# The router's logits as four fp32 products of rows copied as they are, in place of twelve products of fp16 halves

## The chip, the cores and the metric

The kernel runs on one core of one Trainium2 chip. The metric is the device time of one execution in microseconds. Engines are named as the profile names them: PE (TensorE), PEld (its weight loads), DVE (VectorE), ACT (ScalarE), POOL (GpSimd), SP (SyncE); ACTq, POOLq and the like are the instruction queues of these engines.

## The reference, cut to what matters

Two blocks of a transformer on x of 4 x 512 rows of 512 numbers (a sequence mixer, a Hadamard feed-forward, cross-attention over 4 x 1024 context rows, and a mixture of 32 experts of which each row takes 8). The change touches the router of the last part:

```python
x = x + _L1_xattn_ref(_layernorm(x, axis=-1), ctx_2048, mask_BxS2_bk0)
x = x + _L1_ffn_ref(_layernorm(x, axis=-1), L1_ffn_gate_kernel, ...)
...
    x2d = hidden_states.reshape(T, D)                 # T = 2048 rows of D = 512
    router_logits = x2d @ gate_kernel                 # gate_kernel: 512 x 32, fp32
    routing_weights = jax.nn.softmax(router_logits, axis=-1)
    routing_weights, selected_experts = jax.lax.top_k(routing_weights, TOP_K)
    ...
    # rows sorted by expert, gate, up and down products of each expert's rows, weighted sum back
```

## The kernel before, in words

The work is written out by hand, engine by engine, as one program for each engine; only semaphores order one against another. The 2048 rows are 16 tiles of 128 rows (`NT` = 16, `TT` = 4 to each of 4 batches).

From about 612 us on, the cross-attention and the router run in one loop over the tiles. In its turn t the program of PE does, in this order: `probs(t)` (eight transposes of the attention weights, L1848), `logits(t - 2)` (L1827), `scores(t + 1)` (24 products of 128x512), `rank(t - 2)` (three small products, L1839 to L1841), `readout(t)` (24 products of 128x512), with `query_tile` and `router_tile` (four transposes each, L1814) put between its pieces. `router_tile(t - 1)` transposes the normalised rows of tile t - 1 into PSUM. From there ACT writes them to SBUF as fp16 (`router_hi`, L776) and DVE writes what the rounding left, as fp16 too (`router_lo`, L1334). `logits` then is, for each of the four pieces of 128 of the 512 numbers, three products with the high and low halves of the gate matrix (`gkh`, `gkl`), which ACT and DVE make once before the loop (L783, L1395); PE waits for `gkl` before its first scores. A product here is a weight load of 128x128 and a matmul that streams 32 columns.

In the same turn DVE does `probs_lo` (L1306), the root of the layer norm interleaved with the choice of the 8 experts of tile t - 2 (`tile_root_and_choose`, L1012 to L1032 and L1339 to L1367), the normalised rows (L1065), `scores_max(t + 1)` (L1300), `place_first` and `place` (L1381 to L1391, which give the rows' places `POS`), then `query_lo`, `router_lo`, `readout_sum` (L1324). ACT does `probs_hi` (L761), `router_exp` (L780), `exp_tile` (L755), `query_hi`, `router_hi`. POOL waits for `POS` and issues eight scatters of the tile's rows into HBM (L560). The last two tiles (a = 14, b = 15) are written out behind the loop.

From about 872 us on, the experts' loop goes over 159 tiles of rows sorted by expert, 8 tiles to a turn. ACT begins each turn with two loads of a table into registers (`rows_at`, `experts_due`, L104): the places of 12 tiles, and for 16 tiles the count at which their expert has landed. SP writes rows of padding behind the last row of each expert (`pad_expert`, L494) and loads the weights of the experts, four of them at a time (L488).

Of the kernel before, what the change touches and what calls it, by code (L numbers as in the profile page):

```python
# [15 lines left out]
F16 = mybir.dt.float16  # L16
# [90 lines left out]

def wait_apart(eng, sem, value, passed):


    eng.wait_ge(sem, value)
    eng.sem_inc(passed, 1)


def build(nc, a_x, a_ctxT, a_ctxr, a_kv, a_mask, a_winT, a_woutT, a_cols, a_rows, a_wug, a_wdT,
          a_gk, a_exp, a_ident, a_had, a_hadf, a_tri, d_exp, d_kv, d_row, d_down, a_out):
    ctx = ExitStack()
    with ctx:
# [28 lines left out]
        gkh = sb("gkh", [P, KC, NE], F16)  # L147
        gkl = sb("gkl", [P, KC, NE], F16)
# [99 lines left out]
        rh = [f16(SUMX, 0, (KC, P)), f16(HT, 1024, (KC, P))]  # L248
        rl = [f16(SUMX, KC * P // 2, (KC, P)), f16(HT, 1280, (KC, P))]
# [80 lines left out]
        s_rt, s_rhi, s_rlo = sem("router_tile_transposed"), sem("router_tile_hi"), sem("router_tile_lo")  # L330
        s_gkh, s_gkl, s_rc0, s_rcz = sem("router_hi"), sem("router_lo"), sem("router_consts"), sem("row_pads_cleared")
# [20 lines left out]
        def _(sp):  # L352
# [152 lines left out]
            for e in range(WP):  # L505
                pad_expert(e, 16 * e)
            sp.wait_ge(s_tab, 1)
            with sp.Fori(1, NE // WP) as i:
                for h in range(WP):
                    pad_expert(i * WP + h, i * (16 * WP) + 16 * h)  # L510
                    wait_apart(sp, s_wl, i * (16 * WP) + 16 * h, s_spassed)

                    done = sp.value_load(TCUM[0:1, bass.ds(i * WP + (h - WP), 1)], min_val=1, max_val=NTILE + 1)
                    sp.wait_ge(s_ed, done)
                    load_expert(i * WP + h, h)
# [5 lines left out]
        def _(pool):  # L521
# [68 lines left out]
            with pool.Fori(0, LOOPS) as it:  # L590
                start = load_ints(pool, "expert_start", TAB[0:1, 4, bass.ds(it * U, U)], 0, NTILE)
                for u in range(U):
                    add(it * U + u, u, start[u])
            start = load_ints(pool, "last_start", TAB[0:1, 4, bass.ds(LOOPS * U, REST)], 0, NTILE)
# [5 lines left out]
        def _(act):  # L600
# [181 lines left out]
            act.wait_ge(s_gk, 16)  # L782
            act.activation(gkh[:, :, :], gk, ACT.Copy, scale=E_S).then_inc(s_gkh, 1)  # L783
# [9 lines left out]
            for t in range(NT - 1):  # L793
                probs_hi(t)
                if t == 0:
                    for b in range(3, B):
                        count_keys(b)
                if t > 1:
                    router_exp(t - 2)
                exp_tile(t + 1)  # L800
                if t + QA < NT:
                    query_hi(t + QA)
                if t:
                    router_hi(t - 1)
# [3 lines left out]
            for t in range(NT - 2, NT):  # L808
                router_hi(t)
                router_exp(t)  # L810
# [18 lines left out]
            def experts_due(name, t, count):  # L829
                return load_ints(act, name, TAB[0:1, 1, bass.ds(t, count)], 16, 16 * NE)  # L830
# [21 lines left out]
            with act.Fori(0, LOOPS) as it:  # L852
                rows, due = rows_at("tile_row", it * U + 4, U + 4), experts_due("tile_due", it * U, U + 8)
                for u in range(U):
                    t = it * U + u

                    hidden_hi(t, u % 2)
                    tile_hi(t + 2, u % 2, due[u + 2])
                    if u < TOPK - LEAD:
                        act.wait_ge(s_add[LEAD + u], LANDED)  # L860
                    load_tile((u + LEAD) % U, t + (V + LEAD - U + 1), rows[u + LEAD - 4], due[u + LEAD])
                    tile_silu(t + 1, (u + 1) % 2)
# [13 lines left out]
        def _(dve):  # L876
# [166 lines left out]
            def tile_root_and_choose(m, n, cols, t):  # L1043

                tile_root_start(m, n, cols)
                logits_scale(t)
# [322 lines left out]
            def choose(t):  # L1369

                logits_scale(t)
# [22 lines left out]
            dve.wait_ge(s_gkh, 1)  # L1394
            v.scalar_tensor_tensor(gkl[:, :, :], gk, E_S, gkh[:, :, :], ALU.mult, ALU.subtract).then_inc(s_gkl, 1)  # L1395
# [7 lines left out]
            for t in range(NT - 1):  # L1403
# [36 lines left out]
                if t:  # L1440
                    router_lo(t - 1)
# [57 lines left out]
            router_lo(a)  # L1499
            last_moments(1)  # L1500
            root_start(1)
            logits_scale(a)
# [15 lines left out]
            router_lo(b)  # L1518
# [93 lines left out]
        def _(pe):  # L1612
# [247 lines left out]
            pe.wait_ge(s_gkl, 1)  # L1860
# [198 lines left out]
```

## Time and profile before

| | |
|---|---|
| median of 3 runs | 1451.21 us (1450.37 to 1453.27) |
| span of the profiled execution | 1474.3 us |
| PE busy | 1382.7 us (94%) |
| DVE busy | 1022.1 us (69%) |
| ACT, POOL busy | 505.4 us, 383.7 us |
| matmuls, weight loads | 7525, 7526 |
| mean granted TensorE clock | 0.977 |

The profile gives one execution, and its span is the only time that it records for it; it is 23.1 us above the median of the runs that were timed without a profile. Nothing else is known of what lies around the span. A row of the timeline gives start and duration; a matmul's start is a measured time, its end is modelled, so the pace of products is read from start to start. The brackets at a row's end say how long the engine had been idle before it and what ended that.

### The profile page before, as it was taken

What the parts mean: (1) busy time and instruction counts of PE and PEld (TensorE: products, weight loads), DVE (VectorE), ACT (ScalarE), POOL (GpSimd) and SP (SyncE); (2) the same over time, 40 slices, a digit from 0 to 9 for tenths busy, and PEclk for the clock granted to TensorE, in tenths of its full rate; (3) what the DMA queues carried; (4) which work ended last, traced back from release to release, by engine and by line L of the source; (5) the groups of instructions that cost most, each with busy time, mean ns of one, the idle gap of its engine ahead of it and who ended that gap; (6) DMA issues with size and microseconds to landing.
All of it is one profiled execution on the core that took longest, in us unless ns stands there. A gap on an engine that the chain in (4) does not pass through costs nothing.

```text
span 1474.3 us, 26984 instructions
## 1 busy us (share of the span) xinstructions
PE 1382.7 (94%) x7525; PEld 753.2 (51%) x7526; DVE 1022.1 (69%) x2467; ACT 505.4 (34%) x916; POOL 383.7 (26%) x313
## 2 busy tenths in 40 slices
PE   4799999999999999999999559999999999999997
PEld 3344444444444444455444236666666666666664
DVE  7879857976895656688776536666666666666664
ACT  1454543444435343422222113333333333333332
POOL 1000000000000000025556543444344344344443
PEclk9899999999999999999999769999999999999999
DMA  9975776766767778836748668889999888989785
GB/s 370 396 262 193 263 256 213 247 197 205 241 209 237 235 254 286 280 119 251 284 195 294 242 227 216 223 218 260 246 246 234 221 229 228 247 223 222 148 162 84
DMA packets 132696, 345.04 MB, mean 234 GB/s; under 512 B 15008, under 2 KB 19616, under 8 KB 125728
## 3 DMA queue, kind: packets, MB, share of 16 engines
q1 hardware_dynamic: 73488, 206.72, 41.6%
q0 software_dynamic: 34640, 85.74, 25.2%
q10 hardware_dynamic: 24512, 51.89, 10.8%
q8 instruction: 27, 0.44, 0.1%
q14 instruction: 29, 0.24, 0.0%
HBM read 192.68 MB, written 151.62 MB: 234 GB/s over the span
## 4 chain that ended last, share of the span: by engine, by line
PE 68%; DVE 16%; DMA 4%; issue 4%; ACT 3%; another core or an unknown queue 2%; ACTq 1%; SPq 1%; DVEq 0%; POOLq 0%
PE PS L1671 17%; PE PS L1673 17%; PE PS L1672 17%; PE PS L1933 5%; PE PS L1961 2%; PE PS L1962 2%; DMA split_experts<-HT 2%; DMA CST<-in_kv 1%; PE PS L1950 1%; DVE EX L1300 1%; PE PS L1951 1%; DVE EX L1306 1%; DVE nw L1027 1%; DMA X<-in_x 1%
## 5 line engine op out<-in xcount | busy, mean ns | idle before, releaser
L587 POOL DMA_INDIRECT out<-BIG,EX x159 | 247.2, 1555 | 354.9 <-issue 153.4
L1671 PE MATMUL PS<-BIG 128*128 (+1 forms) x795 | 269.5, 339 | 5.0 <-DVE BIG L1572 3.3
L1672 PE MATMUL PS<-BIG 128*128 (+1 forms) x795 | 269.5, 339 | 0.0
L1673 PE MATMUL PS<-BIG 128*128 (+1 forms) x795 | 269.5, 339 | 0.0
L1671 PE MATMUL PS<-HT,BIG 128*128 128x512 f16 (+1 forms) x512 | 194.1, 379 | 3.0 <-DVE HT L1101 1.4
L1672 PE MATMUL PS<-HT,BIG 128*128 128x512 f16 (+1 forms) x512 | 194.0, 379 | 0.0
L1673 PE MATMUL PS<-HT,BIG 128*128 128x512 f16 (+1 forms) x512 | 194.0, 379 | 0.0
L560 POOL DMA_INDIRECT rows_by_expert<-HT,POS x128 | 124.9, 976 | 122.6 <-DVE POS L1391 88.1
L1672 PE MATMUL PS<-BIG,EX 128*128 128x512 f16 (+1 forms) x376 | 143.8, 382 | 1.1 <-issue 1.1
L824 ACT ACTIVATE BIG<-PS 128x256 f16<-128x256 f32 x159 | 61.1, 384 | 243.3 <-PE PS L1951 229.0
L1673 PE MATMUL PS<-BIG,EX 128*128 128x512 f16 (+1 forms) x376 | 143.6, 382 | 0.4 <-issue 0.4
L1671 PE MATMUL PS<-BIG,EX 128*128 128x512 f16 (+1 forms) x376 | 143.8, 382 | 0.0
L1576 DVE SCALAR_TENSOR_TENSOR BIG<-PS,BIG 128x192 f32<-128x192 f32 x159 | 56.8, 357 | 104.1 <-ACT BIG L820 95.1
L1567 DVE SCALAR_TENSOR_TENSOR BIG<-PS,BIG 128x512 f16<-128x512 f32 x159 | 109.9, 691 | 23.8 <-ACT BIG L816 14.0
L1585 DVE TENSOR_SCALAR BIG<-PS,BIG 128x512 f32<-128x512 f32 x159 | 119.4, 751 | 0.0
L650 ACT ACTIVATE HT<-HT 128x1280 f16<-128x1280 f32 x64 | 81.2, 1268 | 94.5 <-DMA split_experts<-HT 94.3
L552 POOL MEMSET HT<- 128x105 f32 x1 | 0.2, 186 | 422.7 <-DMA split_experts<-HT 422.7
L1673 PEld LDWEIGHTS PS<-BIG 128*128 128x128 f16 x795 | 78.3, 98 | 59.6 <-issue 1.6
L820 ACT ACTIVATE BIG<-PS 128x192 f32<-128x192 f32 x159 | 52.7, 331 | 158.4 <-PE PS L1673 133.0
L1933 PE MATMUL PS<-ident,BIG 128*128 128x128 f32 x636 | 96.8, 276 | 7.7 <-issue 7.7
L1671 PEld LDWEIGHTS PS<-BIG 128*128 128x128 f16 x795 | 78.2, 98 | 50.1 <-issue 9.9
L816 ACT ACTIVATE BIG<-PS 128x512 f16<-128x512 f32 x158 | 93.4, 591 | 25.3 <-remote 25.3
(264 smaller groups left out, 2218.0 us busy)
## 6 DMA issues: line engine op xcount, KB each, us to landing
BIG<-rows_by_expert ACTq DMA_DIRECT2D x159, 280.0 KB
HT<-in_experts SPq DMA_DIRECT2D x64, 640.0 KB, 4.6
BIG<-split_experts SPq DMA_DIRECT2D x32, 1152.0 KB
split_experts<-HT SPq DMA_DIRECT2D x96, 320.0 KB, 2.2
CST<-in_kv SPq DMA_DIRECT2D x64, 256.0 KB, 4.7
split_context<-RT SPq DMA_DIRECT2D x64, 256.0 KB, 4.5
BIG<-split_context SPq DMA_DIRECT2D x7, 2048.0 KB
rows_by_expert<-X SPq DMA_DIRECT2D x32, 280.0 KB
```

Source lines behind the costliest of these rows:

```text
L560: pool.indirect_dma_start(d_row, bass.IndirectOffsetOnAxis(ap=POS[:, t % ZN, c:c + 1], axis=0), ZR[:, t % ZN, :], None).then_inc(s_ids[t % ...
L587: pool.indirect_dma_start(a_out, bass.IndirectOffsetOnAxis(ap=IDY[:, u % V:u % V + 1], axis=0), yt[u % V], None, compute_op=ALU.add).then_ ...
L650: act.activation(eoh, est[h], ACT.Copy, scale=E_S).then_inc(s_eh, 1)
L816: act.activation(xh[p], PS[:, p, :].rearrange("p (k n) -> p k n", n=P), ACT.Copy, scale=H_S).then_inc(s_xh, 1)
L824: act.activation(eah[p], PS[:, 4, 0:2 * P], ACT.Copy).then_inc(s_ah2, 1)
L1567: v.scalar_tensor_tensor(xl[p], PS[:, p, :].rearrange("p (k n) -> p k n", n=P), H_S, xh[p], ALU.mult, ALU.subtract).then_inc(s_xl, 1)
L1576: v.scalar_tensor_tensor(ea[p][:, 0:M], PS[:, 2 + p, M:2 * M], 1.0 / (H_S * E_S), eg[p], ALU.mult, ALU.mult)
L1585: v.tensor_scalar(yt[u % V], PS[:, 5 + u % 2, :], xg[u][:, bass.ds(e + D, 1)], None, ALU.mult).then_inc(s_y, 1)
L1671: mm(out, lh, rh, start=first, stop=False)
L1672: mm(out, lh, rl, start=False, stop=False)
L1673: return mm(out, ll, rh, start=False, stop=last_group)
L1933: last = nc.tensor.transpose(PS[:, u % 2, k * P:(k + 1) * P], xg[u][:, k * P:(k + 1) * P], ident[:, :])
```

## The change

The copy of the transposed rows to SBUF stays fp32 (`rx`) and is ACT's alone; DVE's half (`router_lo`) and both halves of the gate matrix go. `logits` is four products with an fp32 stationary operand (`rx`) and an fp32 moving one (`gk`, which lies in the place of `hadf`). The logits are copied from PSUM instead of scaled. Three edits outside the router come with it: ACT and POOL raise the counts that they load into registers to at least their lower bound (`load_counts`), ACT loads them for 12 tiles of a turn instead of 16, and SP writes the padding of experts 4 to 7 before its loop and from there on four experts ahead.

```diff
+def load_counts(eng, name, table, least, most):
+    loaded = [eng.alloc_register(f"{name}{i}") for i in range(table.shape[-1])]
+    held = [eng.alloc_register(f"{name}_held{i}") for i in range(table.shape[-1])]
+    eng.reg_load(loaded, table)
+    for to, of in zip(held, loaded):
+        eng.reg_alu(to, of, least, ALU.max)
...
-        rh = [f16(SUMX, 0, (KC, P)), f16(HT, 1024, (KC, P))]
-        rl = [f16(SUMX, KC * P // 2, (KC, P)), f16(HT, 1280, (KC, P))]
+        rx = [f32(SUMX, 0, (KC, P)), f32(HT, 1024, (KC, P))]
...
-            for e in range(WP):
+            for e in range(2 * WP):
                 pad_expert(e, 16 * e)
             sp.wait_ge(s_tab, 1)
-            with sp.Fori(1, NE // WP) as i:
+            with sp.Fori(1, NE // WP - 1) as i:
                 for h in range(WP):
-                    pad_expert(i * WP + h, i * (16 * WP) + 16 * h)
...
+                    pad_expert(i * WP + (h + WP), i * (16 * WP) + 16 * (h + WP))
+                    replace_expert(i * WP + h, h)
...
-            def router_hi(t):
+            def router_copy(t):
                 last = t == NT - 1
                 act.wait_ge(s_rt, t + 1)
-                act.activation(rh[last], PS[:, 7 - last, :].rearrange("p (k n) -> p k n", n=P), ACT.Copy, scale=H_S).then_inc(s_rhi, 1)
+                act.activation(rx[last], PS[:, 7 - last, :].rearrange("p (k n) -> p k n", n=P), ACT.Copy).then_inc(s_rx, 1)
...
-            act.wait_ge(s_gk, 16)
-            act.activation(gkh[:, :, :], gk, ACT.Copy, scale=E_S).then_inc(s_gkh, 1)
...
-                rows, due = rows_at("tile_row", it * U + 4, U + 4), experts_due("tile_due", it * U, U + 8)
+                rows, due = rows_at("tile_row", it * U + 4, U + 4), experts_due("tile_due", it * U + 2, U + 4)
...
-            def router_lo(t):
-                last = t == NT - 1
-                dve.wait_ge(s_rhi, t + 1)
-                v.scalar_tensor_tensor(rl[last], PS[:, 7 - last, :].rearrange("p (k n) -> p k n", n=P), H_S, rh[last], ALU.mult, ALU.subtract)\
-                    .then_inc(s_rlo, 1)
...
-            def logits_scale(t):
+            def logits_copy(t):
                 dve.wait_ge(s_lg, t + 1)
-                v.tensor_scalar(rlog, PS[:, 7 - (t == NT - 1), 0:NE], 1.0 / (H_S * E_S), None, ALU.mult).then_inc(s_L, 1)
+                v.tensor_copy(rlog, PS[:, 7 - (t == NT - 1), 0:NE]).then_inc(s_L, 1)
...
             def logits(t):
                 last = t == NT - 1
-                pe.wait_ge(s_rlo, t + 1)
+                pe.wait_ge(s_rx, t + 1)
                 for k in range(KC):
-                    done = three(PS[:, 7 - last, 0:NE], rh[last][:, k, :], rl[last][:, k, :], gkh[:, k, :], gkl[:, k, :], k == 0, k == KC - 1)
+                    done = mm(PS[:, 7 - last, 0:NE], rx[last][:, k, :], gk[:, k, :], start=(k == 0), stop=(k == KC - 1))
                 done.then_inc(s_lg, 1)
...
-            pe.wait_ge(s_gkl, 1)
+            pe.wait_ge(s_gk, 16)
             scores(0)
```

PE, between the transposes of `probs(t)` and the scores of the next tile, in every turn from the third on (a product of the list is one call; `hadf` is where `gk` lies, `SUMM` where the rows of the tile lie):

```order
 L1848 MATMUL PS<-ident,EX 128x128 x8
-L1671 MATMUL PS<-gkh,SUMM 128x32
-L1672 MATMUL PS<-gkl,SUMM 128x32
-L1673 MATMUL PS<-gkh,SUMM 128x32
...
+L1831 MATMUL PS<-hadf,SUMM 128x32 x4
 L1671 MATMUL PS<-BIG,HT 128x512
 L1672 MATMUL PS<-BIG,HT 128x512
```

Of the three kinds of rows with a minus there are four each. Nothing else moves on PE.

DVE, from the low half of the query tile to the next tile's `probs_lo`, first before, then of the changed kernel:

```order
L1328 SCALAR_TENSOR_TENSOR HT<-PS,HT 128x4x128 [waits query_tile_hi]
L1334 SCALAR_TENSOR_TENSOR SUMM<-PS,SUMM 128x512 [waits router_tile_hi]
L1317 RECIPROCAL attn<-attn 128x1 [waits probs_ready]
L1319 TENSOR_TENSOR attn<-attn,valid 128x1 [waits sum_inverted]
L1324 SCALAR_TENSOR_TENSOR X<-PS,attn,X 128x512 [waits readout_product,sum_scaled]
L1003 BN_STATS st<-X 128x6 [waits readout_added]
L1005 BN_AGGR mv<-st 128x2 [waits ln_stats]
L1306 SCALAR_TENSOR_TENSOR EX<-PS,EX 128x1024 [waits probs_hi]
```

```order
L1340 SCALAR_TENSOR_TENSOR HT<-PS,HT 128x4x128 [waits query_tile_hi]
L1329 RECIPROCAL attn<-attn 128x1 [waits probs_ready]
L1331 TENSOR_TENSOR attn<-attn,valid 128x1 [waits sum_inverted]
L1336 SCALAR_TENSOR_TENSOR X<-PS,attn,X 128x512 [waits readout_product,sum_scaled]
L1015 BN_STATS st<-X 128x6 [waits readout_added]
L1017 BN_AGGR mv<-st 128x2 [waits ln_stats]
L1318 SCALAR_TENSOR_TENSOR EX<-PS,EX 128x1024 [waits probs_hi]
```

One instruction with its wait is gone, and the others stand as before.

ACT, at the head of each turn of the experts' loop, first before, then of the changed kernel (ISA is a fused group of register operations):

```order
L104 TENSOR_LOAD EX
L104 ISA
L104 TENSOR_LOAD EX
L823 REGISTER_ALU
L824 ACTIVATE BIG<-PS 128x256
L815 REGISTER_ALU
```

```order
L104 TENSOR_LOAD EX
L112 ISA
L112 TENSOR_LOAD EX
L114 ISA x2
L835 REGISTER_ALU
L836 ACTIVATE BIG<-PS 128x256
```

The second load is shorter by four numbers, and two groups of register operations stand behind it, ahead of the copy of the transposed hidden rows.

## Rows read from the trace of the kernel before

**Rows 1.** Stretches: length, busy of PE, PEld, DVE, ACT, POOL, clock, DMA, GB/s.

```profile
81.90:85.40 3.50, 3.50 (x34) 3.46 (x33) 2.05 (x2) 0.40 (x1) 0.00 (x0) 1.00 0.66 250
...
642.54:655.02 12.48, 12.48 (x82) 6.91 (x80) 10.94 (x43) 3.67 (x6) 2.70 (x3) 1.00 0.37 136
709.06:722.73 13.67, 12.68 (x81) 6.82 (x80) 10.50 (x42) 3.56 (x6) 7.82 (x8) 1.00 0.72 261
830.20:860.70 30.50, 10.64 (x66) 6.69 (x67) 14.96 (x74) 1.84 (x4) 17.92 (x19) 0.50 0.71 255
900.00:1000.00 100.00, 100.00 (x625) 63.36 (x624) 66.94 (x163) 32.49 (x81) 38.85 (x25) 1.00 0.88 224
```

**Rows 2.** Timeline of DVE and POOL in one turn of the loop.

```profile
715.49 0.97 POOL L560 DMA_INDIRECT rows_by_expert<-HT,POS  x1 [0.30 <-issue]
716.41 0.16 DVE L1032 SCALAR_TENSOR_TENSOR nw<-nw 128x2 f32<-128x2 f32 x1 [1.09 <-DVE nw L1027]
718.03 1.23 DVE L1300 CUSTOM_DVE_ANT_0 EX<-PS,BIG 128x1024 f32<-128x1024 f32 x1 [0.87 <-remote]
```

**Rows 3.** Waits, 650 to 785 us: who waited for whom, us in total, times, longest.

```profile
DVE EX L1300 <- remote: 8.5, 9, 1.1
PE PS L1814 <- DVE RP L1381: 4.8, 8, 1.0
```

**Rows 4.** Timeline of PE: first of the twelve products, and the two behind the last.

```profile
643.25 0.18 PE L1671 MATMUL PS<-gkh,SUMM 128*128 128x32 f16 x1
...
643.55 0.38 PE L1671 MATMUL PS<-BIG,HT 128*128 128x512 f16 x1
643.77 0.38 PE L1672 MATMUL PS<-BIG,HT 128*128 128x512 f16 x1
```

**Rows 5.** The chain of waits at the fp32 products near the start (start, us).

```profile
73.32 3.43 PE PS L1628 x8
81.94 3.47 PE PS L1619 x32
```

**Rows 6.** The fp32 products of line 1619: counts, ns min/median/max.

```profile
L1619 PE MATMUL PS<-cm,BIG x64: 168/302/373, 14.8 to 85.2; 128*128 128x1 f32 x32, 128*128 128x3 f32 x32
```

**Rows 7.** The same line at the start of the trace, timeline.

```profile
14.82 5.50 PE L1619 MATMUL PS<-cm,BIG 128*128 128x1 f32 x25 [14.82 <-DMA BIG<-in_woutT]
```

**Rows 8.** Groups of lines by shape, 650 to 785 us: count, busy us, mean ns, idle before.

```profile
L1334 DVE SCALAR_TENSOR_TENSOR SUMM<-PS,SUMM 128x512 f16<-128x512 f32 x10 | 6.8, 680 | 0.5 <-ACT SUMM L776 0.5
```

**Rows 9.** ACT's copies of PSUM to SBUF that stay fp32.

```profile
L607 ACT ACTIVATE BIG<-PS x16: 597/597/598, 33.8 to 46.7; 128x512 f32<-128x512 f32 x16
```

**Rows 10.** Timeline at the start of the attention.

```profile
612.02 0.38 PE L1673 MATMUL PS<-BIG,EX 128*128 128x512 f16 x1
612.54 0.39 PE L1671 MATMUL PS<-BIG,HT 128*128 128x512 f16 x1
```

**Rows 11.** Timeline of the last two tiles (14 from 834.62, 15 from 840.59).

```profile
834.62 0.60 ACT L776 ACTIVATE SUMM<-PS 128x512 f16<-128x512 f32 x1 [11.97 <-remote]
...
837.30 0.19 DVE L1339 TENSOR_SCALAR RT<-PS 128x32 f32<-128x32 f32 x1
...
840.59 0.97 POOL L560 DMA_INDIRECT rows_by_expert<-HT,POS  x1 [7.39 <-DVE POS L1391]
840.75 0.60 ACT L776 ACTIVATE HT<-PS 128x512 f16<-128x512 f32 x1 [2.48 <-PE PS L1814]
...
842.66 0.19 DVE L1339 TENSOR_SCALAR RT<-PS 128x32 f32<-128x32 f32 x1 [0.59 <-PE PS L1673]
```

**Rows 12.** Register loads of line 104, 900 to 1460 us.

```profile
L104 ACTq TENSOR_LOAD <-EX x38: 290/1012/2399, 903.4 to 1439.5; - x38
L104 ACTq FUSED_REGOPS  x18: 51/51/51, 904.2 to 1410.9; - x18
```

**Rows 13.** Timeline at the head of a turn of the experts' loop.

```profile
905.81 0.42 DVE L1572 TENSOR_TENSOR BIG<-PS,BIG 128x256 f16<-128x256 f32 x1 [0.90 <-ACT BIG L824]
...
906.53 0.38 PE L1671 MATMUL PS<-BIG 128*128 x1
```

More of the change, by code:

```diff
@@ L105, in load_ints @@
     return [eng.snap(x, donate=True, min_val=least, max_val=most) for x in regs]
+def load_counts(eng, name, table, least, most):
[4 more added lines that the diff above has]
+        eng.reg_alu(to, of, least, ALU.max)
+        eng.free_register(of)
+    return [eng.snap(x, donate=True, min_val=least, max_val=most) for x in held]
 def wait_apart(eng, sem, value, passed):
@@ L146, in build @@
         gk = hadf[:, 0, :].rearrange("p (k e) -> p k e", k=KC)
-        gkh = sb("gkh", [P, KC, NE], F16)
-        gkl = sb("gkl", [P, KC, NE], F16)
         tri = sb("tri", [P, 6, P], F16)
@@ L504, in _, with replace_expert @@
             sp.wait_ge(s_tpad, 2)
-            for e in range(WP):
+            for e in range(2 * WP):
                 pad_expert(e, 16 * e)
             sp.wait_ge(s_tab, 1)
-            with sp.Fori(1, NE // WP) as i:
-                for h in range(WP):
-                    pad_expert(i * WP + h, i * (16 * WP) + 16 * h)
[L511 to L515, printed above, removed]
+            def replace_expert(e, h):
+                wait_apart(sp, s_wl, e * 16, s_spassed)
+                done = sp.value_load(TCUM[0:1, bass.ds(e - WP, 1)], min_val=1, max_val=NTILE + 1)
+                sp.wait_ge(s_ed, done)
+                load_expert(e, h)
+            with sp.Fori(1, NE // WP - 1) as i:
+                for h in range(WP):
+                    pad_expert(i * WP + (h + WP), i * (16 * WP) + 16 * (h + WP))
+                    replace_expert(i * WP + h, h)
+            for h in range(WP):
+                replace_expert(NE - WP + h, h)
             for w in range(V):
@@ L590, in _ @@
             with pool.Fori(0, LOOPS) as it:
[L591 removed]
+                start = load_counts(pool, "expert_start", TAB[0:1, 4, bass.ds(it * U, U)], 0, NTILE)
                 for u in range(U):
                     add(it * U + u, u, start[u])
[L594 removed]
+            start = load_counts(pool, "last_start", TAB[0:1, 4, bass.ds(LOOPS * U, REST)], 0, NTILE)
             for u in range(REST):
@@ L803, in _ @@
                 if t:
-                    router_hi(t - 1)
+                    router_copy(t - 1)
             for n in range(2):
@@ L808, in _ @@
             for t in range(NT - 2, NT):
-                router_hi(t)
+                router_copy(t)
                 router_exp(t)
@@ L829, in experts_due @@
             def experts_due(name, t, count):
-                return load_ints(act, name, TAB[0:1, 1, bass.ds(t, count)], 16, 16 * NE)
+                return load_counts(act, name, TAB[0:1, 1, bass.ds(t, count)], 16, 16 * NE)
             def load_tile(u, used, row, pads):
@@ L857, in _ @@
                     hidden_hi(t, u % 2)
-                    tile_hi(t + 2, u % 2, due[u + 2])
+                    tile_hi(t + 2, u % 2, due[u])
                     if u < TOPK - LEAD:
                         act.wait_ge(s_add[LEAD + u], LANDED)
-                    load_tile((u + LEAD) % U, t + (V + LEAD - U + 1), rows[u + LEAD - 4], due[u + LEAD])
+                    load_tile((u + LEAD) % U, t + (V + LEAD - U + 1), rows[u + LEAD - 4], due[u + LEAD - 2])
                     tile_silu(t + 1, (u + 1) % 2)
@@ L1045, in tile_root_and_choose @@
                 tile_root_start(m, n, cols)
-                logits_scale(t)
+                logits_copy(t)
                 tile_root_half(m, cols, 0)
@@ L1369, in choose @@
             def choose(t):
-                logits_scale(t)
+                logits_copy(t)
                 top8(t)
@@ L1393, in _ @@
             dve.wait_ge(s_rc0, 3)
-            dve.wait_ge(s_gkh, 1)
-            v.scalar_tensor_tensor(gkl[:, :, :], gk, E_S, gkh[:, :, :], ALU.mult, ALU.subtract).then_inc(s_gkl, 1)
             dve.wait_ge(s_mask, 16)
@@ L1498, in _ @@
             last_stats(1, b)
-            router_lo(a)
             last_moments(1)
             root_start(1)
-            logits_scale(a)
+            logits_copy(a)
             root_square(1, 0)
```

7 lines of the change are left out of this document (2 added, 5 removed).

## The prediction, as it was made before the run

> **What bounds the kernel now.** I read busy time by stretch first, then the loop of attention and router turn by turn, then the waits, and last the places at which the other edits act.
>
> By stretch, PE has 100.00 of 100 us in the experts' loop [rows 1], and the small logits are no part of it. The change acts on 612 to 850 us, where the tiles go through attention and router. The first turn there that has logits in it, from the transposes at 642.54 to those at 655.02, takes 12.48 us, and PE is busy for all 12.48 of them, DVE for 10.94 [rows 1]: PE sets the pace. A later turn, 709.06 to 722.73, holds the same work and takes 13.67 us, PE busy 12.68, so PE stands for 0.99 [rows 1]. What it waits for is DVE's `place_first`, L1381, in eight turns of this stretch, 1.0 us at the longest [rows 3]. And DVE is late there because it is held itself. The reader should look at three starts: POOL's last scatter of the tile runs from 715.49 to 716.46, DVE's L1032 has stood idle for 1.09 us and starts at 716.41, and `scores_max` (L1300), idle for another 0.87, starts at 718.03, 1.57 us behind the scatter's end, released by something that the profile can't name [rows 2]. Nine times between 650 and 785 us that release is "remote", 8.5 us in total [rows 3]. The turn at 642.54 had only 2.70 us of POOL in it, the one at 709.06 has 7.82 [rows 1].
>
> So there are two readings of the loop: work on PE, 12.5 to 12.7 us a turn, or a circle through POOL's scatters, 13.7 us, with about 1 us to spare on PE. Which of them holds in the runs that are timed decides this case.
>
> **The change, part by part.**
>
> *PE's products.* The twelve fp16 products begin at 643.25 and the next product at 643.55: 0.30 us a tile, 0.025 each [rows 4]. The fp32 products that the trace has are shown as two weight loads and two matmuls each: line 1619 makes 16 of them a call, and has 64 matmuls for its two calls [rows 6]. Four products are so 8 load-and-matmul pairs. Their price is not in the trace, since no fp32 product there streams 32 columns. The nearest row is line 1619's second call: 32 pairs in 3.47 us, 0.108 each, with the same fp32 128x128 stationary operand and 3 columns streamed [rows 5, 6], at a granted clock of 1.00, which is 2.4 GHz [rows 1]. Its PEld is busy 3.46 of 3.50 us, so the loads fill the time. Line 1628 streams 512 columns, 8 in 3.43 us, 0.43 each [rows 5]; 32 columns in that proportion are 0.027. Lower bound, the columns alone: 8 x 0.027 = 0.21 us a tile, 0.09 less than now. Upper bound, loads and columns one behind the other: 8 x 0.135 = 1.08, 0.78 more. I take 8 x 0.108 = 0.87, 0.57 more, since a load of the same size is what row 1619 shows, and 27 ns of columns fit under a load of 108. By the Trainium skill (FP8 and Floating Point Precision, TensorE Precision Notes) a true fp32 product is four passes through the array; counting columns alone, 4 products x 4 passes x 32 are 512 columns, which at the pace of a 512-column fp16 product would be 0.22 us a tile and make the change a gain of 0.08 on PE. Row 1619 speaks against it: 3 columns took no less than 0.108.
>
> Fourteen of the sixteen tiles' logits stand where PE is the engine at work (tiles 0 to 11 in turns 2 to 13, tiles 12 and 13 between the products of the last turns). If PE sets the pace: 14 x 0.57 = +8.0 us. Bounds: 14 x -0.09 = -1.3 and 14 x 0.78 = +10.9.
>
> *DVE's low half.* 0.68 us a tile is gone [rows 8]. It stands between `place` and `readout_sum`, and `readout_sum` waits for PE's readout. With PE as the pace this pays nothing; nor does it in the circle through POOL, which goes from `scores_max` over `POS` to the scatters and passes by. I take 0.
>
> *ACT's copy.* 0.60 us as fp16 [rows 11], 0.60 as fp32 [rows 9]. Nothing.
>
> *The gate's halves.* PE starts its first score at 612.54, 0.52 us behind the last readout-sized product at 612.02 [rows 10], where these follow each other every 0.22 [rows 4]: 0.30 us of waiting for `gkl`. The gate matrix has landed by then, since ACT has already made `gkh` of it. -0.3.
>
> *The last two tiles.* The clock is at 0.50 from 830.20 to 860.70 [rows 1], that is 1.2 GHz. Tile 14: from ACT's copy at 834.62 to the logits on DVE at 837.30 are 2.68 us [rows 11]; after: copy 0.60, eight pairs at twice 0.108, 1.73 (line 1619 needed 5.50 / 25 = 0.22 in its first call [rows 7]), about 0.08 for two handovers, 2.41: 0.27 earlier. Tile 15: now 1.91 us from 840.75 to 842.66 [rows 11], after 2.41, so 0.50 later, 0.23 in all. POOL waits 7.39 us for tile 14's places and starts at 840.59 [rows 11], then has four scatters of 1.28 to make before it wants tile 15's, so that is covered and the 0.27 counts. Behind this the experts wait for POOL. -0.3.
>
> *The head of an experts' turn.* DVE's low half of the hidden rows ends at 906.23 and PE's down product that needs it starts at 906.53 [rows 13]: 0.3 us of cover there, next to none in others that I looked at. Each 0.1 us more on ACT at the head could so cost up to 19 x 0.1 = 1.9 us. The load of 16 numbers is now one of 12; the median load of ACT, over both sizes, is 1012 ns, a fused group of register operations 51 ns [rows 12]. In proportion four numbers are worth up to 0.25 us, two groups with their gaps cost 0.1 to 0.2. I take 0; bounds -1.9 (it can't gain more than PE waits there) and +3.8. POOL's maxima lie under its waits for DVE. SP's padding ahead: three more transfers of 280 KB before the experts' loop, on a queue from which nothing is wanted then; 0, and at worst 1 us each.
>
> **The sum.** With PE as the pace: 8.0 - 0.3 - 0.3 = +7.4. Against the profiled execution's own time, its span of 1474.3, the sum is another: in the turns with 0.99 us of idle PE, 0.57 disappears, the first turn pays 0.57, the ends give back 0.6, in all 0. The median is 23.1 us below the span, and thirteen turns of 13.67 instead of 12.48 are 15 of these 23. That is why I take it that in the timed runs most of that holding is absent and PE sets the pace. It is an inference; no row shows it. 1451.2 + 7.4 = 1458.6.
>
> **The rivals.**
>
> *The circle through the scatters holds in the timed runs too* (same). Place: L1032 and L1300 behind POOL's scatters. Price: PE's 0.57 goes into its 0.99 of idle time; +0.6 - 0.6 = 0, 1451.2. It decides as long as PE has 0.57 us to spare in a turn. For it: each hold ends with a POOL instruction or a fixed 1.57 behind it. By the Trainium skill (SBUF: State Buffer, on the shared port pair) a DVE instruction with two SBUF inputs fully blocks against a GpSimd instruction that reads SBUF; L1032 is such a one, and by that the hold is of the chip and not of the profile. The row of L1032 agrees (716.41 against 716.46), the 1.57 of L1300 is not explained by it. Against it: the 23.1 us.
>
> *The fp32 products cost only their columns* (same). 14 x -0.09 - 0.6 = -1.9, 1449.3. For it only the page on precision.
>
> *DVE sets the pace* (faster). If in the timed runs PE's products run ahead and DVE's chain closes the circle, each of 13 turns gains 0.68: -8.8 - 0.6, 1441.8. It decides from the point at which DVE's turn exceeds PE's 12.5 to 13.1; the one clean turn shows DVE at 10.94. It would need DVE's waits on its own semaphores to fill 2 us.
>
> *The head of the experts' turn grows* (slower), by 0.2 us in each of 19, with the circle holding: +3.8, 1455.0.
>
> **How the numbers follow.** PE as the pace 0.47, the circle 0.33, cheap products 0.05, DVE 0.10, the head 0.05. A change of less than 0.2% (2.9 us) is about what can't be told from none. Slower: 0.47 + 0.05 = 0.52; same 0.33 + 0.05 = 0.38; faster 0.10. The likeliest case's own range is 1455 to 1462 (10.9 in place of 8.0). The range of the whole, 1449 to 1461.7, leaves out DVE's case and the outer edge of the others.
>
> **What would show it.** In the changed profile: eight matmuls at L1831 in 0.8 to 1.0 us at full clock between the transposes and the scores; the turn that begins near 642 longer by 0.5 to 0.6; the later turns unchanged at 13.7 with PE's wait for L1387 (was L1381) down from 1.0 to about 0.4, and a span within 3 us of 1474.3, while the timed runs rise by 5 to 10. If the timed runs stay too, the circle is real. I am wrong if the pairs pace at 0.03, if turns become shorter, or if PE waits at the head of the experts' turns.

## The result and the profile after

The changed kernel takes 1504.2 us (median of 4 runs, 1502.7 to 1508.6) beside 1450.8 us for the kernel before on the same chip: a ratio of 1.0366, 95% interval 1.0346 to 1.0387. It is slower, by 53.4 us, where 7.4 had been forecast. Its profiled execution has a span of 1501.0 us, 1.8 under the time of the same run; all later runs show this distance too. So the 23.1 us between the span of before, 1474.3, and its median was no cost of profiling: that trace must be of a slower kind of execution than the timed runs, which the seventh experiment comes back to.

The stretches first, two turns of the attention loop, the end of it, and 100 us of the experts' loop (length, busy of PE, PEld, DVE, ACT, POOL, clock, DMA, GB/s):

```profile
644.69:657.69 13.00, 13.00 (x78) 7.44 (x76) 10.24 (x42) 3.67 (x6) 2.71 (x3) 1.00 0.36 123
709.67:722.67 13.00, 13.00 (x78) 7.44 (x76) 9.85 (x41) 3.66 (x6) 7.80 (x9) 1.00 0.68 260
830.00:870.00 40.00, 23.40 (x120) 13.57 (x121) 17.89 (x64) 7.34 (x16) 22.08 (x21) 0.73 0.83 274
900.00:1000.00 100.00, 94.64 (x588) 59.62 (x587) 62.63 (x155) 30.30 (x76) 38.84 (x25) 1.00 0.85 212
```

The first turn is 0.52 us longer than in [rows 1]. The second is shorter than its counterpart there, 13.00 against 13.67, although it holds more work, since PE no longer stands. And PE now stands 5.4 of 100 us in the experts' loop, where it stood for none. That is where most of the time went. The chain of work that ended last says who holds PE there. Around the turn that begins at 915.8 us (start, us, what):

```profile
915.79 0.82 ACTq L104
...
916.72 2.72 ACTq L112
...
919.77 0.39 ACT BIG L836
...
920.19 0.43 DVE BIG L1572
```

ACT's second load of numbers into registers takes 2.72 us. Behind it stand the copy of the transposed hidden rows (L836), DVE's low half of them (L1572) and PE's product, which had been idle for 1.66 us:

```profile
920.75 0.39 PE L1671 MATMUL PS<-BIG 128*128 x1 [1.66 <-DVE BIG L1572]
```

Over the whole loop, the group of L1671 (count, busy, mean ns, idle before and its releaser), and the two loads of ACT (count, duration min/median/max in ns):

```profile
L1671 PE MATMUL PS<-BIG 128*128 (+1 forms) x795 | 271.3, 341 | 39.8 <-DVE BIG L1572 38.1
```

```profile
L112 ACTq TENSOR_LOAD <-EX x21: 941/2842/4295, 839.7 to 1465.9; - x21
```

38.1 us of waiting for DVE's low half, behind a load of 12 numbers whose median is 2.84 us. In [rows 12] the median over both of ACT's loads, of 12 and of 16 numbers, was 1.01. The load now begins at `it * U + 2`; before, it began at `it * U`. Five of the 18 waits at the heads, of 2.2 to 3.2 us, are followed by a lower granted clock (0.50 to 0.78 over the next 2 us), and that costs time beyond the waiting. The length of the wait alone does not decide it: after 2.64 us at 1371 us the next 2 us show 0.50, after 2.89 at 1017 they show 1.00.

### The profile page after: what moved, and what is told of

It is laid out like the page before. It is cut to its first block, busy times and chain, and to the rows that moved or that the text cites. A ratio compares the mean times of both kernels' runs of the same rounds, so it can differ in the third digit from the quotient of the medians.

```text
span 1501.0 us, 26900 instructions
## 1 busy us (share of the span) xinstructions
PE 1397.6 (93%) x7461; PEld 767.1 (51%) x7462; DVE 1011.1 (67%) x2450; ACT 505.2 (34%) x915; POOL 383.3 (26%) x313
## 4 chain that ended last, share of the span: by engine, by line
PE 68%; DVE 12%; DMA 6%; ACTq 5%; issue 4%; ACT 2%; SPq 1%; DVEq 0%; POOLq 0%
PE PS L1671 17%; PE PS L1673 17%; PE PS L1672 17%; PE PS L1933 4%; ACTq L112 4%; DMA CST<-in_kv 3%; PE PS L1962 2%; PE PS L1961 2%; ACTq L104 1%; DMA split_experts<-HT 1%; PE PS L1950 1%; PE PS L1951 1%; DMA X<-in_x 1%; DMA rows_by_expert<-X 1%; PE PS L1848 1%
## 5 line engine op out<-in xcount | busy, mean ns | idle before, releaser
L1671 PE MATMUL PS<-BIG 128*128 (+1 forms) x795 | 271.3, 341 | 39.8 <-DVE BIG L1572 38.1
L1671 PE MATMUL PS<-HT,BIG 128*128 128x512 f16 (+1 forms) x512 | 194.1, 379 | 3.7 <-DVE EX L1119 1.6
L836 ACT ACTIVATE BIG<-PS 128x256 f16<-128x256 f32 x159 | 60.9, 383 | 293.3 <-PE PS L1951 208.1
L1671 PE MATMUL PS<-BIG,EX 128*128 128x512 f16 (+1 forms) x376 | 143.0, 380 | 0.0
L1572 DVE TENSOR_TENSOR BIG<-PS,BIG 128x256 f16<-128x256 f32 x159 | 67.4, 424 | 92.1 <-ACT BIG L836 91.0
L1671 PEld LDWEIGHTS PS<-BIG 128*128 128x128 f16 x795 | 78.7, 99 | 89.0 <-issue 50.0
```

The source lines that it names most:

```text
L836: act.activation(eah[p], PS[:, 4, 0:2 * P], ACT.Copy).then_inc(s_ah2, 1)
L1572: v.tensor_tensor(eal[p], PS[:, 4, 0:2 * P], eah[p], ALU.subtract).then_inc(s_al2, 1)
L1671: mm(out, lh, rh, start=first, stop=False)
```

## The experiments

All runs that take a part of the change alone use `load_counts` for ACT's due times; the kernel of the run `maxima` is their base. Each time stands beside the kernel before on the same chip. Kernels compared with one another below ran on one chip, unless it is said.

**1. The parts, one by one.** Theory A: the changed start of the load. Theory B: the register operations behind it. `maxima` is the kernel before with these alone:

```diff
-                return load_ints(act, name, TAB[0:1, 1, bass.ds(t, count)], 16, 16 * NE)
+                return load_counts(act, name, TAB[0:1, 1, bass.ds(t, count)], 16, 16 * NE)
```

> The kernel before with one part of the change: the loaded numbers of ACT's due times and of POOL's starts go through a maximum (load_counts), still 16 numbers from it * U. Theory A (the changed start of ACT's load of due times costs about 2 us at each of 20 turn heads): no change, 1449 to 1454 us. Theory B (the maxima, a register operation for each number right behind the load, are what costs): 1485 to 1500 us.

Measured: 1453.4 us beside 1451.0, ratio 1.0026 (1.0014 to 1.0037). The operations cost 2.4 us here and 1.3 when the run was repeated (`maxima2`, below); theory B falls.

```diff
-                rows, due = rows_at("tile_row", it * U + 4, U + 4), experts_due("tile_due", it * U, U + 8)
+                rows, due = rows_at("tile_row", it * U + 4, U + 4), experts_due("tile_due", it * U + 2, U + 4)
```

> The kernel of the run maxima, with ACT's load of due times from it * U + 2 (12 numbers) in place of it * U (16 numbers). Theory A: 20 heads at 2.0 to 2.3 us each over the kernel before, so 1490 to 1497 us, and in the trace L112 on ACT's queue near 2.6 us beside 1.0. Theory B: the same as the run maxima, within 3 us of it. Theory C (the heads are late for the loop of attention turns, or for the pads that SP clears ahead, and not for the load): no change from the kernel before.

Measured: 1498.5 us, ratio 1.0336 (1.0291 to 1.0382), 1.5 above what theory A gave: 45.1 us over `maxima` for a load that is four numbers shorter. The load and PE's group in the experts' loop, of `maxima`, then both of `only_start`:

```profile
L112 ACTq TENSOR_LOAD <-EX x21: 772/1021/2249, 830.5 to 1414.4; - x21
```

```profile
L1682 PE MATMUL PS<-BIG 128*128 x772 | 260.1, 337 | 3.2 <-DVE BIG L1583 3.2
```

```profile
L112 ACTq TENSOR_LOAD <-EX x21: 1053/2850/5336, 833.5 to 1463.7; - x21
```

```profile
L1682 PE MATMUL PS<-BIG 128*128 x753 | 255.2, 339 | 39.7 <-DVE BIG L1583 39.6
```

L1682 and L1583 are here what L1671 and L1572 are in the changed kernel. The load's median is longer by 1.83 us, which 19 times is 35, and PE's waiting for DVE's low half is longer by 36.4; the granted clock over 880 to 1430 us is 0.98 in place of 1.00, which is some 11 us more if PE's work follows it. `only_router` has the fp32 products and copies, and neither the new start nor SP's new order:

> The kernel before with the router's products in fp32 and its copies as in the change (and the maxima); the load of 16 numbers from it * U and SP's order of pads as before. My sum: PE sets the pace of the attention turns, 14 tiles at 0.5 to 0.57 us plus nothing else, so +7 to +8 us, 1457 to 1460. Rival (the stall behind POOL's scatters holds the turn, and PE's added time goes into it): no change, 1449 to 1454. Rival (what the whole change lost was lost here): over 1480.

Measured: 1462.2 us, ratio 1.0090 (1.0059 to 1.0121), 8.7 over `maxima`: my sum had 7.4, and the range of this expectation ended at 1460. `start_back` is the changed kernel with that one load undone:

> The changed kernel with one part undone: ACT loads 16 numbers from it * U again. Theory A: the loss at the heads goes, 40 to 46 us of the 53, so 1457 to 1464 us. Theory B or C: still above 1490 us.

Measured: 1461.4 us, ratio 1.0078 (1.0053 to 1.0103). The heads' loss is gone, 43 us of it (against the 1504.2 of the first set of runs), and its load is back at a median of 1047 ns. PE's wait for DVE's low half falls from 38.1 to 5.0 us. The parts add up: 1450.8 + 2.4 + 8.7 + 45.1 = 1507, beside the 1504.2 and, in the last experiment, 1508.1 of the whole.

**2. SP's padding ahead**, alone on `maxima`.

> The kernel of the run maxima with SP's order of the change: the pads of 2 * WP experts ahead, and those of expert i + WP in the loop. The pads are not what PE waits for in the experts' loop, and the start of the experts' part moves little: 1451 to 1456 us, no different from the run maxima by more than 2 us. Rival: the longer chain of pads ahead of the first experts' tiles delays them, 1456 to 1462.

Measured: 1453.6 us beside 1452.6, ratio 1.0009 (0.9997 to 1.0021). Nothing.

**3. The other load of the same turn**, moved to a start of the same kind.

```diff
-                rows, due = rows_at("tile_row", it * U + 4, U + 4), experts_due("tile_due", it * U, U + 8)
+                rows, due = rows_at("tile_row", it * U + 2, U + 6), experts_due("tile_due", it * U, U + 8)
```

> The kernel of the run maxima with ACT's other load of the turn changed: the row numbers come from it * U + 2 (14 numbers) in place of it * U + 4 (12 numbers); the due times from it * U as before. Theory A (any load of ACT at the head whose start is 2 above a multiple of 8 costs 2 us more): 1453 + 20 x 2.2 = 1490 to 1503 us. If the loss belongs to the due times alone: 1451 to 1456.

Measured: 1527.9 us beside 1452.6, ratio 1.0535 (1.0513 to 1.0557). It isn't the due times: any load of this place does it. But 74.5 us over `maxima` (run on another chip, whose kernel before took 1451.0) is far more than expected. The load explains 19 x (3.16 - 0.87) = 44 us (its median against that of `maxima`); PE waits 50.5 us for DVE's low half, 47 more than there. The rest is put down to the clock: where PE had stood for 3.5 us at a head, it comes back at 0.50, which is 1.2 GHz:

```profile
L104 ACTq TENSOR_LOAD <-EX x21: 292/3162/5095, 829.9 to 1489.3; - x21
```

```profile
915.98 0.60 PE L1682 MATMUL PS<-BIG 128*128 x1 [3.54 <-DVE BIG L1583]
```

```profile
916.00:918.00 2.00, 2.00 (x5) 0.85 (x6) 0.99 (x3) 0.17 (x1) 0.00 (x0) 0.50 0.59 159
...
880.00:1430.00 550.00, 502.33 (x2963) 313.79 (x2961) 318.66 (x775) 155.38 (x389) 203.71 (x132) 0.95 0.84 201
```

After 15 of the 18 waits at the heads the next 2 us show a clock below 1.00. Over 550 us of the loop the mean clock is 0.95, a loss of some 27 us in 550 if the products follow it, and 47 and 27 are the 74.5; the changed kernel has 0.99 there, the run `start_back` 1.00.

**4. What makes a load slow.** The first two attempts gave nothing: unused loads, and loads whose sum was held to a constant, were left out of the program by the compiler.

> The kernel of the run maxima with 28 further loads into 16 registers of ACT that nothing uses, once, ahead of the experts' loop, each on its own line (L853 to L880): 4 numbers of the due times from 0, 1, 2, 3, 4, 6, 8, 12 and 16; 12 numbers from 0, 2, 4, 8, 1, 6, 32 and 34; 1 number from 0 and 2; 2 numbers from 0, 2 and 1; 8 numbers from 0, 2 and 4; 16 numbers from 0, 2 and 4. Theory A1 (a load whose start is no multiple of four numbers is slow): 12 numbers take 0.8 us from 0, 4, 8 and 32 and 2.6 us from 1, 2, 6 and 34; 4 numbers some 0.4 us from a multiple of four and 1 us or more from the others; one number 0.29 us from anywhere. Theory A2 (only a start that is a multiple of eight is quick): the start of 4 is as slow as that of 2. Theory A3 (the load was slow because of what stood beside it in the experts' loop, not by its start): all of one count take the same.

> The run loads again, but with every loaded number added up and the sum (held to 16) waited on, so that the loads can't fall away: 29 loads on ACT ahead of the experts' loop, of 4 numbers from 0, 1, 2, 3, 4, 6 and 8; of 12 from 0, 2, 4, 8, 1, 3, 6 and 34; of 1 from 0 and 2; of 2 from 0, 2 and 1; of 8 from 0, 2 and 4; of 16 from 0, 2 and 4; of 3, 5 and 10 from 0. The time of the kernel says nothing here, only each load's duration. Theory A1 (slow from any start that is no multiple of four): 12 numbers 0.8 us from 0, 4 and 8, 2.6 us from 1, 2, 3, 6 and 34. Theory A2 (quick from multiples of eight alone): the start of 4 as slow as that of 2. Theory A3 (the start makes no difference outside the loop): 12 numbers take the same from all eight starts. If the cost is one of single numbers, about 0.25 us each: 4 numbers from 2 near 1.1 us, 16 from 2 near 3.9 us.

Measured: no such instruction in either trace (1459.4 and 1452.2 us, one run each, beside 1452.6 and 1449.6 for the kernel before). `loads` shows something else, though: its load of 16 numbers from `it * U`, the same as in `maxima`, has a median of 1.50 us in place of 1.02, and PE's wait for DVE's low half is 9.3 us in place of 3.2.

```profile
L112 ACTq TENSOR_LOAD <-EX x21: 845/1500/3340, 832.9 to 1422.7; - x21
```

So the start is not all that a load in the loop depends on; what made these longer stays open. The third attempt has the loads:

```diff
+            act.reg_load(probe[:12], TAB[0:1, 1, 2:14])
+            add_up(total, probe[:12])
...
+            act.reg_alu(total, total, 32, ALU.min)
+            act.reg_alu(held, total, 16, ALU.max)
+            act.wait_ge(s_pad, act.snap(held, donate=True, min_val=16, max_val=32))
```

> The 29 loads of the run loads_used once more, now behind the first two loads of rows and due times (L864 to L920), with the sum held between 16 and 32 so that it isn't a constant. The kernel's time says nothing here, only each load's duration. Theory A1 (slow from any start that is no multiple of four): 12 numbers 0.8 us from 0, 4 and 8, 2.6 us from 1, 2, 3, 6 and 34; 4 numbers near 0.4 us from 0, 4 and 8 and near 1 us from the others; 1 number 0.3 us from 0 and 2 alike. Theory A2 (quick from multiples of eight alone): the start of 4 as slow as that of 2. Theory A3 (outside the loop the start makes no difference): all starts of one count alike.

Measured (durations in ns; each load is one row, measured once): 12 numbers from 2, from 8, from 34; 4 from 0, 1, 2 and 4; 12 from 0 and from 4; 1 from 0, 2 from 0; 8 from 2 and 4; 16 from 0 and 2; 10 from 0.

```profile
L880 ACTq TENSOR_LOAD <-EX x1: 2929/2929/2929, 868.5 to 868.5; - x1
L884 ACTq TENSOR_LOAD <-EX x1: 783/783/783, 872.9 to 872.9; - x1
L892 ACTq TENSOR_LOAD <-EX x1: 2587/2587/2587, 882.8 to 882.8; - x1
L864 ACTq TENSOR_LOAD <-EX x1: 315/315/315, 857.9 to 857.9; - x1
L866 ACTq TENSOR_LOAD <-EX x1: 2174/2174/2174, 858.4 to 858.4; - x1
L868 ACTq TENSOR_LOAD <-EX x1: 1370/1370/1370, 860.7 to 860.7; - x1
L872 ACTq TENSOR_LOAD <-EX x1: 318/318/318, 863.6 to 863.6; - x1
L878 ACTq TENSOR_LOAD <-EX x1: 1225/1225/1225, 866.3 to 866.3; - x1
L882 ACTq TENSOR_LOAD <-EX x1: 500/500/500, 872.1 to 872.1; - x1
L894 ACTq TENSOR_LOAD <-EX x1: 285/285/285, 885.7 to 885.7; - x1
L898 ACTq TENSOR_LOAD <-EX x1: 500/500/500, 886.5 to 886.5; - x1
L906 ACTq TENSOR_LOAD <-EX x1: 1764/1764/1764, 889.3 to 889.3; - x1
L908 ACTq TENSOR_LOAD <-EX x1: 554/554/554, 891.2 to 891.2; - x1
L910 ACTq TENSOR_LOAD <-EX x1: 1022/1022/1022, 892.0 to 892.0; - x1
L912 ACTq TENSOR_LOAD <-EX x1: 3432/3432/3432, 893.4 to 893.4; - x1
L920 ACTq TENSOR_LOAD <-EX x1: 1005/1005/1005, 900.2 to 900.2; - x1
```

Theory A1 holds: a start of 4 is as quick as one of 0 or 8 (4, 8 and 16 numbers from 4 took 0.32, 0.55 and 1.02), and 12 numbers from 1, 3 and 6 took 2.82, 2.60 and 2.58 us. From a start off the fours, 16 numbers take 3.43, 12 take 2.59, 8 take 1.76: 0.22 us a number. From a multiple of four, 4, 8, 12 and 16 take 0.32, 0.55, 0.78 and 1.02: 0.24 us for each further four. 10 numbers from 0 are 1.01, two fours and two single numbers (0.55 + 2 x 0.22 = 0.99). These figures are those of the loads from 877 us on, and of 4 from 0 and 4, 12 from 8. Most of the earlier ones don't fit: 4 numbers from 1, 2, 3 and 6 took 2.17, 1.37, 1.28 and 1.34 where 0.22 each gives 0.88, 4 from 8 took 0.58, 12 from 0, 1 and 2 took 1.23, 2.82 and 2.93, and 12 from 4 took 0.50. POOL's scatters still ran up to 869 us; whether they are the reason was not tested. All these loads go into the same registers, so it isn't the registers that differ, and the experts' loop hasn't begun, so the slowness needs nothing of the loop. The page DMA: Bandwidth & Descriptors of the Trainium skill (Latency and other measured facts) gives `tensor_load` a floor near 600 ns and says that the compiler unrolls it by four; durations that go by fours agree with that, the floor doesn't show (285 ns for one number), and the page has nothing on the start.

**5. Fourteen numbers from `it * U`**, in the changed kernel, two of them thrown away.

```diff
-                rows, due = rows_at("tile_row", it * U + 4, U + 4), experts_due("tile_due", it * U + 2, U + 4)
+                rows, due = rows_at("tile_row", it * U + 4, U + 4), experts_due("tile_due", it * U, U + 6)
```

> The changed kernel with ACT's due times from it * U, and 14 numbers of them (the two below the first that is needed are thrown away) in place of 12 from it * U + 2. If the start alone is at fault and the count isn't: within 3 us of the run start_back (16 numbers from it * U, 1461.4), 1457 to 1464 us. If a count that is no power of two, or no multiple of four, is slow: 1485 us or more.

Measured: 1485.0 us, but beside a kernel before that took 1480.4 on this chip, ratio 1.0031 (1.0017 to 1.0044). The count is not at fault: the load's median is 1252 ns, three fours and two numbers (0.78 + 0.44 = 1.22). The comparison with 1461.4 fails, for a reason that experiment 7 takes up.

**6. Can ACT's loads be hidden?** They stand ahead of `hidden_hi`, which needs no register. In the run `late` they are read behind it:

```diff
                     hidden_hi(t, u % 2)
+                    if u == 0:
+                        due = experts_due("tile_due", it * U, U + 8)
                     tile_hi(t + 2, u % 2, due[u + 2])
+                    if u == 0:
+                        rows = rows_at("tile_row", it * U + 4, U + 4)
```

> The kernel of the run maxima with ACT's two loads moved inside the turn: the due times are read behind the first hidden_hi, the row numbers behind the first tile_hi, since the copy hidden_hi needs no register. If the load stands on the path from ACT through hidden_hi and DVE's hidden_lo to PE's products at the head, as the theory has it, the head's pitch of 4.6 us falls towards 3.7, 19 heads at 0.3 to 0.9 us: 1435 to 1448 us. Rival (tile_hi is then late for PE by as much, or PE's and DVE's own loads hold the head): 1449 to 1456 us.

> The run late with the due times from it * U + 2 (12 numbers). If the slow load costs what it is late on ACT, and tile_hi has some slack where hidden_hi had none: less than the 45 us of the run only_start against maxima, 5 to 25 us over the run late. If tile_hi has no slack: 35 to 45 us over it. If the load costs more than its own time (by something that it holds elsewhere): 45 or more.

Measured: 1469.0 us (ratio 1.0118, 1.0095 to 1.0141) and 1528.1 us (1.0526, 1.0490 to 1.0562). The theory missed in both: `late` lost time, and `late_start` took 59.1 us over `late`, where 5 to 25 had been expected and only the last branch, 45 or more, fits. The wait at the old place is all but gone, and a larger one stands at PE's next transposes, which wait for DVE's gated rows (of `late`, then of `late_start`; L1685 and L1586 are the places of L1671 and L1572, L1964 and L1591 those of L1950 and L1577):

```profile
L1685 PE MATMUL PS<-BIG 128*128 x791 | 267.1, 338 | 1.1 <-DVE BIG L1586 1.1
...
L1964 PE MATMUL PS<-ident,BIG 128*128 128x128 f32 x159 | 44.7, 281 | 23.0 <-DVE BIG L1591 23.0
```

```profile
L1964 PE MATMUL PS<-ident,BIG 128*128 128x128 f32 x159 | 45.7, 288 | 56.1 <-DVE BIG L1591 56.1
```

L1591 needs the result of ACT's `tile_silu`. That stands behind both loads as before, but the loads now begin only behind the first `hidden_hi`, while the matmuls that feed `tile_silu` run: at the head near 912 us of `late` the last of these starts at 910.03 and `tile_silu` at 911.70. There is no slack on ACT for a late load; the old place, where PE's last products of the tile before still ran, was the better one. Of the 59.1 us between the two runs 33.1 are PE's longer wait at L1964; the clock over 880 to 1430 us is 0.95 in `late_start` and 1.00 in `late`, some 27 us if the products follow it. Neither kernel beats the kernel before, and no run here does.

**7. What paces the fp32 products, and which chip shows it.** `twice` does each tile's four fp32 products two times over.

> The kernel of the run only_router with each tile's fp32 products done twice (the second pass starts the sum anew, so the logits are the same). If PE sets the pace of the attention turns, 14 tiles x 0.82 us on top of 1462, and some for the last two: 1472 to 1476 us. If a stall elsewhere would have held the turn with fp32 products too, less than half of that: 1462 to 1467.

Measured: 1477.2 us, 15.0 over `only_router` (1462.2, on another chip with nearly the same time of before, 1451.0 against 1452.6). The expectation had ended at 1476. Its turns are 13.89 us against 13.00: 0.89 us more each, with PE busy throughout. `cols64` streams 64 columns:

```diff
-                    done = mm(PS[:, 7 - last, 0:NE], rx[last][:, k, :], gk[:, k, :], start=(k == 0), stop=(k == KC - 1))
+                    done = mm(PS[:, 7 - last, 0:2 * NE].rearrange("p (a e) -> p a e", a=2), rx[last][:, k, :],
+                              gk[:, k:k + 1, :].to_broadcast([P, 2, NE]), start=(k == 0), stop=(k == KC - 1))
```

> The kernel of the run only_router (1462.2 us) with every fp32 product of the logits streaming 64 columns, the 32 of the router twice over, in place of 32; the logits are read from the first 32. If the pace of 0.11 us of a record is set by what stands between the products (the loads of the fp32 weights), not by the columns: 1460 to 1464 us. If it is set by the columns: the eight records take 1.6 us in place of 0.82, 14 x 0.8 = 11 us more, 1471 to 1475 us.

Measured: 1483.0 us, on the chip where the kernel before took 1480.4: a ratio of 1.0016 (0.9997 to 1.0034), no different. No run of `only_router` stood beside it, and neither branch of the expectation can be read from it. On that chip 19 runs of the kernel before took 1476 to 1486 us; the others ran it in 1447 to 1455. The trace of `aligned14` there is that of [rows 1 to 3] over again: after a first turn of 13.00 us, turns of 13.7 to 13.8 with PE idle in them, and DVE's `scores_max` released by "remote":

```profile
DVE EX L1312 <- remote: 7.0, 8, 1.0
```

```profile
666.00:679.70 13.70, 13.13 (x76) 7.35 (x75) 10.46 (x43) 3.50 (x7) 7.82 (x8) 1.00 0.90 317
```

`cols64` has turns of 13.8 to 13.9 us there behind a first of 13.02, and so has `loads_kept`, which keeps the fp16 products of before, behind a first of 12.48: with the holding in it, the turn doesn't get longer by the fp32 products. So a last set of four was run together, to have the router's part, the pace and the whole on one chip:

> The run maxima again, as the base for the other runs of this call on one chip. Where the attention turns of the kernel before take 12.48 us (its time 1451): 1451 to 1456 us. Where they take 13.7 to 13.8 us (its time near 1480): 1480 to 1485.

> The run only_router again. Where the kernel before shows 12.48 us turns: 13.00 us turns and +7 to +10 us over maxima2. Where it shows 13.7 us turns: the turn is held by the stalls of DVE and PE during POOL's scatters and not by PE, the turns stay at 13.7 to 13.8 and the time within 4 us of maxima2.

> The run cols64 again, beside only_router on the same chip: fp32 products that stream 64 columns in place of 32. If the pace of the records (0.11 us) is set by what stands between the products, the same as only_router2 within 3 us, and turns of 13.0 us where those are 13.0. If by the columns, 11 us more and turns of 13.8.

> The changed kernel again, on the same chip as the three others. Where the kernel before takes 1451: 1500 to 1508 us. Where it takes 1480: the router's part is hidden, the heads' part is not, so 1480 + 45 = 1520 to 1535 us, a ratio near 1.03.

Measured, beside a kernel before of 1451.0: 1452.4 (ratio 1.0010, 1.0000 to 1.0021), 1461.9 (1.0070, 1.0053 to 1.0087), 1460.9 (1.0062, 1.0046 to 1.0079) and 1508.1 us (1.0385, 1.0364 to 1.0406). One turn each of `maxima2` and `only_router2`, with POOL at its scatters (the starts of ACT's copy are 12.48 and 13.00 us apart, ten times over):

```profile
653.30:665.80 12.50, 12.50 (x81) 6.90 (x79) 10.96 (x44) 3.68 (x7) 8.21 (x10) 1.00 0.75 289
```

```profile
654.60:667.60 13.00, 13.00 (x77) 7.43 (x75) 10.26 (x44) 3.67 (x7) 8.27 (x10) 1.00 0.75 280
```

And the products in the chain, of `only_router2`, `twice` and `cols64_2`, whose L1825 is L1831 of the changed kernel:

```profile
644.90 0.81 PE PS L1825 x8
```

```profile
646.11 1.71 PE PS L1825 x16
```

```profile
645.55 0.84 PE PS L1825 x8
```

Twice the columns cost 0.03 us in 0.81 and nothing in the time; twice the products cost 0.90. The pace, 0.10 us a pair of load and matmul, is not the columns'. By the four passes of the page FP8 and Floating Point Precision (TensorE Precision Notes of the Trainium skill), counted as columns alone, an estimate is 0.43 us a tile for 64 columns and 0.22 for 32; the trace has 0.84 and 0.81, so the four passes do not give the price of so narrow a product.

## Why the prediction was wrong

**The step that failed** is "The head of an experts' turn". It had the place right (ACT's loads, with next to no cover before PE's down product), and nearly the price per 0.1 us of delay: up to 1.9 us was said, and `only_start` shows 36.4 / 18.3 = 2.0 of waiting, 45.1 / 18.3 = 2.5 in all, since the clock was not in the sum. What was wrong is the load: "In proportion four numbers are worth up to 0.25 us". I priced it by its count and never by its start. From `it * U + 2` none of its 12 numbers goes by fours; its median is 2.85 us, 1.8 more than that of 16 numbers from `it * U`, and with the slower clock behind the longer waits this costs 45.1 us over the 19 heads, where the outer bound was +3.8. The order printed for ACT could not show it, since an address stands in none of its rows; the diff did. The rival "the head of the experts' turn grows" named the place with a chance of 0.05 and a price twelve times too small.

**PE's products** were right in their mechanism: 0.57 us a tile was said, the turns grew by 0.52; eight pairs take 0.81 us, 0.87 was said. In all the router's part cost +8.7 and +9.5, where 7.4 was said. That this is so near is partly luck: from ACT's copy of tile 0 to that of tile 14 `maxima2` takes 172.99 us and `only_router2` 179.89, so the products cost 6.9 there and not 8.0 (one of these 14 turns, 13.94 us before and 13.90 after, doesn't grow). The rest came at places where the sum had nothing or a gain. The rival of cheap products fell.

**PE as the pace** in the timed runs held, and its argument was half right: the 23.1 us did show that the timed runs lacked the holding. But it doesn't come and go with the profiler. On one chip every timed run of the kernel before is as long as if it had it (1476 to 1486 us), and the three traces taken there show it. There `cols64`, the router's part with 64 columns, costs 2.6 us, beside 9.9 on the last chip, and all that `aligned14` changes costs 4.6, beside 10 for `start_back` on another. So the rival of the circle through the scatters is real there. `only_router` itself was not run on it. Only one set of runs was of this kind, so whether it belongs to the chip or to that occasion isn't told apart, and what sets it apart stays open: no release by "remote" stands among the waits of `maxima2` from 650 to 785 us, although POOL is as busy in its turns (8.21 us above, 7.82 in [rows 1]).

**DVE's low half** paid nothing, as said: DVE is down from 10.96 to 10.26 us a turn with PE busy throughout, and the rival that DVE sets the pace fell. **The maxima** cost 1.3 and 2.4 us, not 0. **The gate's halves**: PE's wait of 0.21 us for them in `maxima2` is gone in `only_router2`, as said, and too small to see in the sum. **The last two tiles**, from copy to logits: in `only_router2` tile 14 takes 1.76 us against 2.18 in `maxima2` (0.42 less, 0.27 said), tile 15 2.60 against 1.91 (0.69 more, 0.50 said). From tile 14's logits to the first hidden copy of the experts' part 31.3 us pass in place of 29.9 (31.0 in `only_router`, 30.6 in `start_back`, 30.1 in `maxima`); I had seen no loss there, and its cause stays open. **SP's padding**: 0, as said.

## What to carry to other kernels

Price a load of numbers into registers by its start before its count: here 12 numbers took 0.8 us from a multiple of four (from 8) and 2.6 to 2.9 from each other start tried, so loading two numbers too many from a whole four is the cheaper form, above all at the head of a loop where an in-order queue has the load ahead of its first real instruction. In a chain without slack a longer wait can also mean a slower clock afterwards: a load longer by 2.3 us a turn cost 3.9. And where the span of a profile and the timed runs differ by more than the 2 us that all later runs here show, they may be executions of two kinds: look for the rows that only one of them can have before a sum is made on either.

## What the runs showed of the hardware that was not expected

- A register load (TENSOR_LOAD on ACT) took, in the later rows of `loads_kept`, 0.24 us for each further four numbers from a start that is a multiple of four, and 0.22 us for each single number from the other starts tried; one number alone took 0.27 and 0.29. Neither is a fixed price: the same load of 16 numbers from `it * U` took 1.01 to 2.25 us in `maxima`, and a median of 1.50 in `loads`.
- Where PE stood for 3.5 us at a head of the run `rows_start`, the granted clock of the next 2 us was 0.50; where it stood for 1.66 in the changed kernel, it stayed at 1.00, and so it did behind one wait of 2.89, but not behind one of 2.64 (0.50).
- fp32 products with a 128x128 stationary operand go at 0.10 us a pair of load and matmul whether 32 or 64 columns stream.
- The same kernel took 1450 to 1453 us on four chips and 1480 on another, in one set of runs each; the traces have a difference in the attention turns during POOL's scatters (12.48 us in `maxima2`, 13.8 to 13.9 in `loads_kept`, which keeps the same products).
